# One post-norm decoder kernel: the row maxima of the first cross attention turned inside a shared PSUM bank, short steps spread, and the last feed-forward network reordered at both ends

## The reference, cut to what matters

```python
def _L0_xattn_ref(x, cross_input, ...):          # 16 heads of 8 channels
    att  = einsum('bhqd,bhkd->bhqk', q, k) * scale         # own keys: 256, causal
    y    = einsum('bhqk,bhkd->bhqd', softmax(where(causal, att, -inf)), v)
    attc = einsum('bhqd,bhkd->bhqk', qc, kc) * scale       # context keys: 1601
    y    = y + einsum('bhqk,bhkd->bhqd', softmax(attc), vc)
    return y.transpose(0, 2, 1, 3).reshape(...) @ Wp + bp

def _L1_ffn_ref(x, ...):                         # 128 -> 512 -> 512 -> 512 -> 128
    h = silu(_tlin(x, w1_w, w1_s)) * _tlin(x, w2_w, w2_s)
    h = gelu(_tlin(h, h1_w, h1_s), approximate=False)
    h = gelu(_tlin(h, h2_w, h2_s), approximate=False)
    return _tlin(h, w3_w, w3_s)

x = _layernorm(x + _L0_attn_ref(x, ...))
x = _layernorm(x + _L0_xattn_ref(x, ctx_512, ...))         # first cross attention
x = _layernorm(x + _L0_ffn_ref(x, ...))                    # mixture of 8 experts, 2 per token
x = _layernorm(x + _L1_attn_ref(x, ...))                   # gated linear recurrence
x = _layernorm(x + _L1_xattn_ref(x, ctx_512, ctx_512, ...))# second cross attention, one head
x = _layernorm(x + _L1_ffn_ref(x, ...))                    # last network
```

## Time and profile before

| | |
|---|---|
| median of 3 runs | 692.98 us (692.75 to 695.24) |
| the profiled execution | 695.09 us, of which the span of the profile is 692.1 us |
| mean granted TensorE clock | 0.974 |
| PE busy | 610.8 us (88%), 5182 matmuls |
| DVE busy | 526.6 us (76%) |
| ACT busy | 449.9 us (65%) |
| POOL busy | 205.5 us (30%) |
| HBM traffic | 100 GB/s over the span |
| the exponential of a bank (L962) | 480 of 0.582 us, started every 0.55 us |
| turning the maxima (L727) | 16 of 0.27 us |
| a float32 product of 128 columns in the second cross attention (L1762) | 16 of 0.275 us |
| gate product (L2258), its high part (L2262), its low part on POOL (L1682) | 0.75, 0.43 and 1.28 us |
| exponential of a norm chunk (L137) at the end | 2 in 1.15 us |

### The profile page before, as it was taken

The page is one execution under the profiler, slowest core; times in us unless marked ns, Lnnn a source line. Parts: engine busy times, 40 slices in busy tenths (PEclk is TensorE's granted clock), DMA queues, the critical chain, the costliest instruction groups (busy, mean ns, idle before and its releaser), DMA issues. The chain is left out here.

```text
span 692.1 us, 13555 instructions
## 1 busy us (share of the span) xinstructions
PE 610.8 (88%) x5182; PEld 332.9 (48%) x5183; DVE 526.6 (76%) x706; ACT 449.9 (65%) x813; POOL 205.5 (30%) x277
## 2 busy tenths in 40 slices
PE   8989899999999999999999874999819899888996
PEld 5645433333333333433333353788304566547883
DVE  5369889999999999999964463899589668767442
ACT  3556578888888888888887451556782256655324
POOL 7224532335455576676640030000000000014000
PEclk9999989999999999999999997999978999999999
DMA  8258575655666544333310069553000100000000
GB/s 206 98 152 278 167 214 182 145 121 140 163 165 159 141 112 98 92 82 89 91 37 2 6 227 408 162 159 111 1 0 0 43 4 0 2 1 0 1 0 30
DMA packets 43293, 70.74 MB, mean 102 GB/s; under 512 B 12492, under 2 KB 31652, under 8 KB 42720
## 3 DMA queue, kind: packets, MB, share of 16 engines
q1 hardware_dynamic: 31696, 38.34, 20.9%
q0 software_dynamic: 10928, 29.32, 13.1%
q10 hardware_dynamic: 608, 2.25, 1.4%
HBM read 44.41 MB, written 24.79 MB: 100 GB/s over the span
## 5 line engine op out<-in xcount | busy, mean ns | idle before, releaser
L962 ACT ACTIVATE prob<-ps 128x512 f32<-128x512 f32 (+2 forms) x480 | 253.1, 582 | 46.2 <-PE ps L738 39.1
L1083 DVE TENSOR_REDUCE pm<-ps 128x2 f32<-128x1024 f32 x192 | 226.0, 1216 | 6.6 <-PE ps L700 4.8
L761 PE MATMUL ps<-prob,vst 128*9 128x256 f32 (+1 forms) x1664 | 130.1, 385 | 10.1 <-ACT o_all L950 10.1
L738 PE MATMUL ps<-qq,kc 50*128 50x256 bf16 (+1 forms) x832 | 134.1, 275 | 0.1
L700 PE MATMUL ps<-kc,qq 48*128 48x512 bf16 x384 | 116.1, 387 | 3.2 <-DVE pm L1083 2.9
L738 PEld LDWEIGHTS ps<-qq,kc 50*128 50x128 bf16 (+1 forms) x832 | 52.2, 96 | 94.2 <-ACT prob L962 69.7
L761 PEld LDWEIGHTS ps<-prob,vst 128*9 128x9 f32 (+1 forms) x1664 | 25.1, 88 | 51.7 <-ACT prob L962 39.1
L1090 DVE TENSOR_REDUCE nm<-ps 128x4 f32<-128x512 f32 (+1 forms) x32 | 30.7, 958 | 14.9 <-PE ps L688 14.9
L1677 POOL DMA_DIRECT2D w_w<-in_w x2 | 1.1, 534 | 137.2 <-PE ps L1716 137.2
L700 PEld LDWEIGHTS ps<-kc,qq 48*128 48x128 bf16 x384 | 32.9, 93 | 13.3 <-DVE pm L1083 9.4
L688 PE MATMUL ps<-masks_b 64*128 64x256 bf16 x256 | 37.6, 269 | 0.0
(11 more groups left out here) (365 smaller groups left out, 1267.2 us busy)
## 6 DMA issues: line engine op xcount, KB each, us to landing
kc<-kc_scr SPq DMA_DIRECT2D x32, 300.2 KB, 4.9
comb_bc<-comb_scr SPq DMA_DIRECT2D x7, 512.0 KB, 4.8
below<-rden_scr POOLq DMA_DIRECT2D x13, 256.0 KB, 6.8
ctx<-ctx_scr POOLq DMA_DIRECT2D x1, 3204.0 KB, 17.0
raw<-in_wexp POOLq DMA_DIRECT2D x8, 384.0 KB, 3.5
exp_scr<-raw_high POOLq DMA_DIRECT2D x8, 384.0 KB, 3.9
exp_scr<-raw_low POOLq DMA_DIRECT2D x8, 384.0 KB, 4.9
kc_scr<-hi SPq DMA_DIRECT2D x6, 400.2 KB, 4.8
```

The source lines that it names most:

```text
L738: last = pe.matmul(bank[0:p, j * TQ:(j + 1) * TQ], kc[s][rows, j, t * 128:t * 128 + p], qq[s][rows, 0, j, :], start=(j == 0), stop=True, s ...
L761: last = pe.matmul(o_ps[32 * hh:32 * hh + VW, kind * TQ + q0:(kind + 1) * TQ], value[:, hh * VW:(hh + 1) * VW], prob[0:k, (NST * n + t) % ...
L962: act.activation(prob[0:p, g % P_RING, 2 * e:2 * e + 2, q0:TQ], s2[0:p, k % S2_RING, 0:2 * w].rearrange("p (i q) -> p i q", i=2), ACT.Exp, ...
L1083: dve.tensor_reduce(pm[:, m % 2, c, :, jt], banks, AX.X, ALU.max).then_inc(s1_read, 1)
```

## The change

It has three parts.

1. **The maxima.** `TURN` loses its own ring numbers, but for the last unit. The turned maxima of unit m - 1 are now written by PE as an ordinary matmul with the identity into columns 384 to 511 of the bank that the half in position 1 of unit m uses, and that half is now the short one, 12 (260 columns). `half_at` maps positions to halves: unit 0 as before; unit 1 has 12 in position 1; from unit 2 on 12 is in position 1, 13 in position 7, and 14 in position 11. DVE reads the turned rows (`row`) just before it reduces position 1. A unit takes 15 ring numbers.
2. **The copy.** `copy_out` stands behind the third exponential of the next unit, where it stood behind the fourth.
3. **The last network.** `ln5` chunk 0 moves to batch 2 (PE: mean after pair 4, variance after pair 5; ACT's square after pair 5, its logarithm and exponential after pair 0 of batch 3; DVE after pair 1 of batch 3), and two weight pieces are split elsewhere. The first layer gets a bank table of its own (`UP`, `UP_FREED`), DVE makes the gate product of tile 0 before it divides in batch 3, and PE does `up(1)`, `up(2)`, the mean of chunk 1, `up(3)`, the variance, then the second layer's tiles 0 and 1 part by part as the low parts come, and only then `up(4)` to `up(7)`. At the end the last layer and `ln6` go in three pieces of 512, 256 and 256 tokens; the first piece and its layer-norm matmuls stand between tiles 5, 6 and 7 of the third layer. The output goes in three DMAs.

```diff
+HALF_AT = ((0, 1, 2, 3, 4, 5, 6, 7, 8, 9, 10, 11, 12, 13, 14),
+           (0, 12, 1, 2, 3, 4, 5, 6, 7, 8, 9, 10, 11, 13, 14),
+           (0, 12, 1, 2, 3, 4, 5, 13, 6, 7, 8, 14, 9, 10, 11))
+TURN_AT, TURN_COLUMNS = 1, slice(384, 512)
...
             for m in range(NU):
-                s1_order.append((m, 0))
-                if m:
-                    s1_order.append((m - 1, TURN))
-                s1_order += [(m, i) for i in range(1, HALVES)]
+                s1_order += [(m, i) for i in range(HALVES)]
             s1_order.append((NU - 1, TURN))
...
                     def turn_maxima(m):
-                        n = s1_at[m, TURN]
-                        wait_s1_free(pe, n)
+                        last = m == NU - 1
+                        n = s1_at[m, TURN] if last else s1_at[m + 1, TURN_AT]
+                        if last:
+                            wait_s1_free(pe, n)
                         pe.wait_ge(nm_ready, m + 1)
-                        pe.transpose(s1[0:16, n % 2, 0, 0:128], nm[:].rearrange("p e k i -> p (e k i)"), ident).then_inc(s1_ready, 1)
+                        pe.matmul(s1[0:16, n % 2, 0, TURN_COLUMNS], nm[:].rearrange("p e k i -> p (e k i)"), ident,
+                                  start=last, stop=True, skip_group_check=True).then_inc(s1_ready, 1)
...
-                            if t == 1 and e == 1 and n:
+                            if t == 1 and e == 0 and n:
                                 copy_out(n - 1)
...
                         for i in range(HALVES):
+                            if m and i == TURN_AT:
+                                row(m - 1)
                             reduce_half(m, i)
-                            if m and i == 0:
-                                row(m - 1)
...
-        UP, H1, H2, Y = ((0, 2), (4, 5), (6, 7)), (1, 3), (6, 7), (0, 2)
+        UP = ((0, 2), (4, 5), (1, 3), (0, 2), (1, 3), (6, 7), (0, 2), (1, 3))
+        UP_FREED = (None, None, None, 1, 3, None, 4, 5)
+        H1, H2 = (4, 5, 0, 2), (6, 7)
+        ends = [slice(0, CH), slice(CH, CH + CH // 2), slice(CH + CH // 2, 2 * CH)]
...
-                        if b == NB - 1 and p == 0:
+                        if b == NB - 2 and p == 4:
                             pe.wait_ge(s1_red, 2 * NB)
                             pe_ln5(0)
-                        if b == NB - 1 and p == 2:
+                        if b == NB - 2 and p == PAIRS - 2:
                             pe_ln5_v(0)
...
+                up(1)
+                up(2)
+                pe_ln5(1)
+                up(3)
+                pe_ln5_v(1)
+                pe.wait_ge(full_done, 2)
+                for i in range(NM):
+                    pe.wait_ge(ha_done, i + 1)
+                    for k in range(2):
+                        done = hidden_part("h1w", ha, H1[k], k, i)
+                        if i == NM - 1:
+                            done.then_inc(h1_ps, 1)
+                for k in range(NM, len(tiles)):
                     up(k)
+                for k in range(2, len(tiles)):
+                    first_hidden(k)
                 pe.wait_ge(split, split_by["h2w"])
-                hidden("h2w", hb, hb_done, H2, g2_done, h2_ps)
...
+                for k in range(6):
+                    second_hidden(k)
+                last_layer(0)
+                second_hidden(6)
                 pe_ln(0)
+                second_hidden(7)
+                pe_ln2(0)
+                last_layer(1)
+                last_layer(2)
                 pe_ln(1)
-                pe_ln2(0)
+                pe_ln(2)
                 pe_ln2(1)
+                pe_ln2(2)
...
                 act.preload_act_table_set("natural_log")
-                act_ln(0)
+                act_log(0)
                 act_ln(1)
-                act_log(0)
+                act_ln(2)
                 act_log(1)
+                act_log(2)
                 act.preload_act_table_set(EXP_LN)
                 act_exp(0)
                 act_exp(1)
+                act_exp(2)
...
                     dve.tensor_copy(osb[:, b % 2, :], o_ps[:, 0:TQ]).then_inc(o_sb, 1)
+                    if b == NB - 1:
+                        gated(0)
```

More of the change, by code:

```diff
@@ L112, in ln_parts @@
                 stack, *[f"{tag}_{n}" for n in ("centred", "squared", "var", "lnv", "rstd", "x")])
+            columns = spans or [slice(c * CH, (c + 1) * CH) for c in range(NCH)]
+            if not spans:
+                psum_c, psum_v = ([p[:, c, :] for c in range(p.shape[1])] for p in (psum_c, psum_v))
             def pe(c):
                 nc.tensor.wait_ge(r_ready, c + 1)
-                nc.tensor.matmul(psum_c[:, c, :], mean_out, R[:, c * CH:(c + 1) * CH],
+                nc.tensor.matmul(psum_c[c], mean_out, R[:, columns[c]],
                                  start=True, stop=True).then_inc(centred, 1)
@@ L120, in pe2 @@
                 nc.tensor.wait_ge(squared, c + 1 - first)
-                nc.tensor.matmul(psum_v[:, c, :], averager, sq[:, c * CH:(c + 1) * CH],
+                nc.tensor.matmul(psum_v[c], averager, sq[:, columns[c]],
                                  start=True, stop=True).then_inc(var_ready, 1)
@@ L1667, in _ @@
             def _(sp):
-                for c in range(NCH):
+                for c, end in enumerate(ends):
                     sp.wait_ge(x_ready, c + 1)
-                    sp.dma_start(out[:, c * CH:(c + 1) * CH], X[:, c * CH:(c + 1) * CH]).then_inc(stored, 16)
-                sp.wait_ge(stored, 16 * NCH)
+                    sp.dma_start(out[:, end], X[:, end]).then_inc(stored, 16)
+                sp.wait_ge(stored, 16 * len(ends))
             @block.gpsimd
@@ new lines, in last_layer @@
+                def last_layer(n):
+                    end = ends[n]
+                    c = end.start // CH
+                    at = slice(end.start - c * CH, end.stop - c * CH)
+                    for i in range(NM):
+                        pe.wait_ge(hc_done, NM * c + i + 1)
+                        done = passes(Y[n], (high_w["w3"][:, i, :], low_w["w3"][:, i, :]), 0,
+                                      [part[:, i, at] for part in hc[c]], i == 0, i == NM - 1)
+                    done.then_inc(y_ps, 1)
```

154 lines of the change are left out of this document (84 added, 70 removed).

## The result

The kernel after takes 674.37 us (median of 4 runs, 668.97 to 680.26), the kernel before 694.11 (4 runs, 692.75 to 695.89); the ratio is 0.969 (0.961 to 0.976). Runs over 1.5% above the fastest of the same kernel, here 680.26, are counted as slow ones and stand in the medians but outside the ratios. A second set of six runs gave 672.41 and 0.968 (0.965 to 0.971). The prediction was 677.4, range 670 to 687. Eleven other kernels were run; the table at the head of the experiments lists them.

A forecast was written before the change was run, and what follows sets the result against it. It took DVE, idle behind short halves, to bound the first cross attention unit, with the network's end second. Terms -10.5 - 0.5 - 2.5 - 4.0 + 0.3 + 1.3 + 2.1 - 1.8 = -15.6 us gave 677.4, range 670 to 687.

The forecast's parts named there:

- The maxima, 14 x 0.75 = 10.5: First cross attention, units 2 to 15: moving the turn and short halves saves 0.75 us a unit, 10.5 us.
- The floor of the new unit is therefore DVE's 17.48 us: First cross attention: DVE's unit of 18.67 us less 1.19 us idle time bounds the new unit.
- My position account: First cross attention: PE's lead over DVE by position; 0.44 us idle at half 13, unit 17.92 us.
- The copy: First cross attention: copy ready 0.55 us earlier, about 0.13 of PE's 0.68 us wait stays; last unit -0.5 us.
- The unit stays bound elsewhere: Rival, first cross attention: mutual waits of ACT and PE set the pace; half the gain, 4.9 us, total 683; chance 0.25.
- All of it comes back: Rival, first cross attention: unit reaches 17.48 us and the norm's waits vanish; 16.7 us gained, total 671; chance 0.13.
- The end gives nothing: Rival, last network: 3.4 us added before the last pass meet a waiting head; network 0, total 682; chance 0.07.
- The row DMAs, chance 0.05: Rival, first cross attention: row DMAs land late, each unit waits 1.4 us, +19.6 us, total 697; chance 0.05.
- My estimate of 4.75 us: Row DMAs, first cross attention: 2.75 us issue plus 2.0 us fixed cost, inside the 5.4 us available.
- Second cross attention, 2.5: Second cross attention: variance matmul moves to batch 2 and PE's 1.45 us stop in batch 3 goes; -2.5 us.
- The head, 4.0 less 0.3: Start of last network: shorter PE stops save 2.3 us, full clock 1.7; the wait of `first_hidden(2)` adds 0.3.
- The term of +1.3 for passes of 256 columns: End of last network: 24 passes of 256 columns at 0.168 us replace 12 of 512 at 0.224; +1.3 us.

The follow-up runs named there:

- without the spread: The kernel after with short halves 13 and 14 kept at the end of units 2 to 15, half 12 at position 1: 675.52 us, ratio 0.972 to before.
- part 3 alone: The kernel before with only the changes to the second cross attention and last network: 687.99 us, ratio 0.990 to before.
- the kernel with the transfers behind the rows: The kernel after with POOL's list reordered, its large stores and broadcast waiting until the row DMAs have landed: 668.91 us, ratio 0.963 to before.
- after once more: The unchanged kernel after, measured again in six runs: 672.41 us, ratio 0.968 to before.
- the transfers on the rows: POOL's reordered list as in the kernel with the transfers behind the rows, but waiting only for the turned rows, not the landing: 684.56 us, ratio 0.987 to before.
- one half more ahead: The kernel after with the maxima one half further ahead (`S1_LEAD` 8 instead of 7): 682.60 us, ratio 0.985 to before.

## Why the prediction was right, and where not

*The total.* 15.6 us forecast against 695.09, 22.9 in the profiled execution (672.2): the direction, the order of the parts and the range held, the size was too small by a third. By the marks the 22.9 us are: 2.3 by the start of the units of full length (I had taken 0; PE's waits for the maxima there, 1.9 us, went too), 11.0 in the 14 units (9.9 in 13 by the marks, 1.1 in the last; forecast 10.5), 1.4 from there to the layer norm (0.5), 0.8 in the mixture of experts and the recurrence, which the change does not touch (0), 2.8 in the second cross attention (2.5), 3.4 in the network (2.1), and 1.2 outside the span (0). That the largest term is nearly right is luck: two errors of 5 us cancel in it, as follows.

*The maxima, 14 x 0.75 = 10.5.* The step that failed is "The floor of the new unit is therefore DVE's 17.48 us": the unit without the spread takes 17.41. DVE's busy time in the earlier trace rows is 242.1 / 14 = 17.29, and it fell to 16.98 without a change in its list; why is open. I read the idle stretches of DVE as losses, though they stop nobody: the 3.3 us were DVE waiting, and in the units only PE's weight loader waited for the ring, 0.2 us each. The loss was where PE kept ACT from its exponentials. PE's stops of 1.24 us a unit became 0.22, ACT's stop behind the turn went from 1.12 to 0.15, and the period fell by 1.15: 13 x 1.15 = 14.9 us, where I had 9.75. My position account gave the idle stretch of 0.40 rightly, and it was worth nothing.

*The copy.* A wait of 0.13 was forecast and 0.22 came; alone it is 0.34 us a unit.

*The rivals on the unit.* "The unit stays bound elsewhere" (0.25) named the mechanism, mutual waits of ACT and PE, but took it for a reason to halve the gain; these waits were what the change removed. "All of it comes back" (0.13) had the unit, 17.48 against 17.53, by DVE's floor and so for a wrong reason. "The end gives nothing" is summed wrongly: -15.6 + 2.1 is -13.5, and its -11 leaves out the second cross attention as well.

*The row DMAs, chance 0.05.* The rival was right in mechanism, in part: not in every unit, but three times in this profile, one of them ahead of unit 0. The other two returned 5.05 us (0.77 + 4.28) of the 14.9, and in the profile of the second set two units were 0.5 and 3.2 us longer. The price I gave it, 1.4 us from a landing of 6.8 us, was too low for one stop: the landing was 8.3 us, and the slower clock behind the stop of 2.86 cost 1.4 more; that it comes in every unit was wrong. "These four carry 2 KB each" was no argument: POOL's transfers of 8 KB `below<-o_all` took a median of 5.2 us from issue to landing between 90 and 358 us of after (4.0 before). What I had missed is that POOL's order against the rows is not fixed, but hangs on its chain fitting into the unit.

On that, the Trainium skill, "DMA: Bandwidth & Descriptors", section "Queues, rings and completion order", has each DMA engine take turns between queues by whole packets; that agrees with small transfers late beside large ones, while no run here shows why the same neighbours delay one unit's rows and not another's. My estimate of 4.75 us took that page's fixed cost for DMAs issued on GpSimd, while the row DMAs are SP's; a landing of 4.3 was dated here (238.17 to 242.45).

*Second cross attention, 2.5.* Measured 2.8, in part 3 alone too. The stop of 1.45 is gone.

*The head, 4.0 less 0.3.* The stop before the mean of chunk 1 was 0.61 instead of 1.1, that of the second layer 0.33 as forecast, the clock 1.00 throughout.

*The end.* The term of +1.3 for passes of 256 columns was mis-sized: 24 x 0.12 = 2.9 us against 12 x 0.224 = 2.7, and one wait of 0.2 for a low part (659.18 to 659.50): +0.4. The row I took the earlier trace rows is four matmuls of another kind, in the cross attention; why those take 0.168 is not shown. I had written that this row decides against the formula of the Trainium skill, "TensorE: Matmul & The Clock Gate", section "Back-to-back issue gap" (0.109 us, 2.6 us in all); the trace is nearer the formula. The two layer-norm matmuls before the last pass cost 0.86 us each from start to start, not 1.06: +1.7 instead of +2.1. Behind the last pass 1.4 us were won instead of 1.8: from there to the end of the last multiplication it takes 6.45 us (661.40 to 667.85) instead of 6.0, and to the end of the program 9.0, above my 8.3 to 8.7. Head and end together gave 3.4 us; my terms sum to 2.1.

## What to carry to other kernels

An engine's busy and idle time always add up to the period, so ask another question: in each kind of step, which engine never stands still, and who waits for whom? Here that was ACT in the plain steps and PE at the turn and the masks, and DVE's idle time was worth nothing, however well its causes were known. When a loop gets shorter, look for the engine whose own chain no longer fits; it does not slow the loop, it slides against it, and its transfers end up beside ones that had been alone. A stop of three or four microseconds on PE cost half as much again here (2.86 us made 4.28, 3.92 made 6.3), since the clock was lower behind it.

## What the runs showed of the hardware

- Four DMAs of 2 KB each landed 4.3 to 4.4 us behind their first issue where a semaphore of the kernel with the transfers behind the rows dates it (119.86 - 115.46, 137.37 - 132.99, 242.45 - 238.17). Behind four stops of PE of 2.1 to 3.9 us they took 7.6 to 9.7 us (244.64 - 237.07 in after once more, 245.79 - 237.45 in after, 159.91 - 150.51 with the transfers on the rows, 249.53 - 239.88 with one half more ahead), and two stores of 384 KB and the 256 KB broadcast of another queue had been issued from 2.6 us ahead of them to 1.7 us behind. The same neighbours also passed without harm.
- PE stops of 2.86 and 3.92 us were followed by 4 and 6 us at 0.56 and 0.50 of the clock.
- fp32r passes of 256 columns, each with its weight load, start every 0.12 us; those of 512 columns every 0.23.
- PE's busy time for the same matmuls in a unit was 17.19 to 17.42 us, and it read 100% in steps with and without 1024 of their columns: it holds waits that it does not show.
- ACT's exponentials of 128 x 512 in a row start every 0.545 us (12 in 6.54).
